# A decoder's feature attention on one Trainium2 core: its products, statistics, stores and loads at other places of a turn, and identity products ahead of stages

## The reference

```python
def _L0_xattn_ref(q, k, v, W):              # q = layernorm(x); k = v = context
    qh = q.reshape(B, H, D, T)              # B 32, H 8 heads, D 8 rows, T 256 features
    kh, vh = ...                            # likewise
    a = jnp.einsum('bhdq,bhdk->bhqk', qh, kh) * D ** (-0.5)
    p = jax.nn.softmax(a, axis=-1)
    y = jnp.einsum('bhqk,bhdk->bhdq', p, vh).reshape(B, C, T)
    return jax.nn.selu(jnp.einsum('oc,bct->bot', W, y))
...
x = x + _L0_attn_ref(_layernorm(x), ...)                 # differential attention
x = x + _L0_xattn_ref(_layernorm(x), ctx, ctx, L0_xattn_W)
x = x + _L0_ffn_ref(_layernorm(x), ...)                  # selection; with the next one: one stage
x = x + _L1_attn_ref(...)                                # state space
x = x + _L1_xattn_ref(...)                               # grouped attention
x = x + _L1_ffn_ref(...)                                 # mixture of experts
```

## Time and profile before

| | us |
|---|---|
| median of three runs | 1376.31 (1371.81 to 1380.15) |
| the profiled execution, its own time | 1374.74 |
| its span, first to last instruction | 1373.0 |
| differential attention | 252 |
| feature attention | 242 |
| selection and state space | 176 |
| grouped attention | 401 |
| mixture | 302 |

### The profile page before, as it was taken

The page is one execution under the profiler, slowest core; times in us unless marked ns, Lnnn a source line. Parts: engine busy times, 40 slices in busy tenths (PEclk is TensorE's granted clock), DMA queues, the critical chain, the costliest instruction groups (busy, mean ns, idle before and its releaser), DMA issues. The chain is left out here.

```text
span 1373.0 us, 27662 instructions
## 1 busy us (share of the span) xinstructions
PE 1233.1 (90%) x9996; PEld 969.6 (71%) x9996; DVE 984.6 (72%) x1869; ACT 704.0 (51%) x1457; POOL 455.3 (33%) x537
## 2 busy tenths in 40 slices
PE   3999998799888957889779999999997799999998
PEld 3776766243333346779658888887876799999998
DVE  4799987688888647788568677777776648555555
ACT  1565655288778835300255656566664363333332
POOL 1333543144554223456562323232422111112210
PEclk9999999699999989899899999999999899999999
DMA  5111026114333130000400000000000300000001
GB/s 178 31 28 35 25 64 136 28 53 110 86 98 94 36 110 1 1 0 0 137 11 4 8 4 8 4 8 4 7 1 0 93 24 25 24 24 24 2 1 62
DMA packets 64927, 54.52 MB, mean 40 GB/s; under 512 B 9192, under 2 KB 56904, under 8 KB 64456
## 3 DMA queue, kind: packets, MB, share of 16 engines
q1 hardware_dynamic: 64846, 53.42, 13.9%
HBM read 38.32 MB, written 14.68 MB: 39 GB/s over the span
## 5 line engine op out<-in xcount | busy, mean ns | idle before, releaser
L783 DVE TENSOR_REDUCE fa_neg_max<-psum 128x2 f32<-128x512 f32 x256 | 161.8, 684 | 26.6 <-PE psum L950 25.7
L838 ACT ACTIVATE fa_probs<-psum 128x1024 f32<-128x1024 f32 x128 | 130.9, 1024 | 37.0 <-PE psum L955 36.8
L1802 PE MATMUL psum<-mo_xT_high,mo_w_high 128*128 128x256 f32 x512 | 145.6, 284 | 2.4 <-DVE mo_xT_low L2630 2.2
L1802 PE MATMUL psum<-mo_xT_low,mo_w_high 128*128 128x256 f32 x512 | 145.2, 284 | 0.0
L1802 PE MATMUL psum<-mo_xT_high,mo_w_low 128*128 128x256 f32 x512 | 144.6, 282 | 0.0
L2462 ACT ACTIVATE mo_silu<-psum 128x256 f32<-128x256 f32 x128 | 49.0, 384 | 155.0 <-PE psum L1802 155.0
L2596 DVE TENSOR_TENSOR mo_mid<-mo_silu,psum 128x256 f32<-128x256 f32 x128 | 53.6, 419 | 92.9 <-ACT mo_silu L2462 92.8
L950 PE MATMUL psum<-stacks_k_stack,stacks_q_stack 48*128 48x256 bf16 x512 | 95.6, 287 | 22.3 <-DVE fa_neg_max L783 15.5
L1802 PEld LDWEIGHTS psum<-mo_xT_high,mo_w_high 128*128 128x128 f32 x512 | 97.4, 190 | 3.0 <-DVE mo_xT_low L2630 2.6
L1938 POOL TENSOR_TENSOR ga_probs<-ga_probs,ga_top 128x1024 f32<-128x1024 f32 x16 | 30.5, 1905 | 205.7 <-DVE ga_top L2092 205.7
L1802 PEld LDWEIGHTS psum<-mo_xT_low,mo_w_high 128*128 128x128 f32 x512 | 97.5, 190 | 0.0
(11 more groups left out here) (419 smaller groups left out, 3586.8 us busy)
## 6 DMA issues: line engine op xcount, KB each, us to landing
k_parts<-da_k_parts SPq DMA_DIRECT2D x96, 64.0 KB, 2.0
q_parts<-stacks_parts SPq DMA_DIRECT2D x96, 64.0 KB, 2.0
stacks_q_stack<-q_parts SPq DMA_DIRECT2D x32, 192.0 KB, 4.0
stacks_k_stack<-k_parts SPq DMA_DIRECT2D x32, 192.0 KB, 3.3
x<-in_x SPq DMA_DIRECT2D x4, 512.0 KB, 5.7
da_context<-in_ctx SPq DMA_DIRECT2D x4, 512.0 KB, 7.8
fa_context<-in_ctx SPq DMA_DIRECT2D x16, 128.0 KB, 2.2
staged<-in_ga_w_q SPq DMA_DIRECT2D x1, 2048.0 KB, 10.5
```

The source lines that it names most:

```text
L783: nc.vector.tensor_reduce(neg_max[:, b, :, head_at(h)], ps[:, h % 2, :].rearrange("p (q k) -> p q k", q=2), AX.X, ALU.max, negate=True).th ...
L838: nc.scalar.activation(probs[:, g].rearrange("p h k q -> p h (k q)"), ps[:, 2 + 2 * (g % 2):4 + 2 * (g % 2), :], ACT.Exp).then_inc(exp_don ...
L1802: done = nc.tensor.matmul(out, lhsT[i], rhs[j], start=start and k == 0, stop=stop and k == 2)
```

## The change

Seven things change, five of them in the feature attention:

1. SP's queue in a turn: context, maxima rows of tile t (second half), then the **stores** of tile t + 3, then the maxima rows of tile t + 1 (first half), then the **loads** of tile t + 2.
2. Queries are stored once per part, three DMAs instead of six, and loaded with three DMAs per lane (of 24, 16 and 8 rows), six instead of two. The keys keep six stores and two loads. The stack in SBUF is the same. The first four tiles, in the differential attention, are stored and loaded likewise.
3. PE: the output product one pair of heads later, the second mixing product one pair of heads later, `turn_mixed(t, 0)` one pair of heads later. ACT's reading of the output product and its copy for `turn_mixed` move with them; ACT now also waits for POOL's selu sum of the turn before.
4. DVE: the statistics one turn later and within the maxima, `normalise` behind the turn's first two maxima, `divide(t, 0)` two maxima later.
5. New: `keep_clock`, products of the identity with itself into a PSUM bank that is overwritten before it is read: 6 ahead of the state-space stage's first transposes, 5 ahead of the grouped attention's, 11 and 14 ahead of the query transposes of its tiles 0 and 1, and in the mixture 5 ahead of its first transposes and 4 behind them.

```diff
+def keep_clock(core, bank, count):
+    for _ in range(count):
+        core.nc.tensor.matmul(core.psum[:, bank, 0:P], core.ident[:], core.ident[:], start=True, stop=True)
...
     def load_q(self, sp, tile, slot, done):
-        self.load(sp, "q_parts", self.q_stack, tile, slot, done)
+        of = self.dram["q_parts"][:, bass.ts(tile, 2 * C_HEADS), :].rearrange("p (b l h) f -> p b l (h f)", b=2, l=LANES)
+        for lane in range(LANES):
+            first = LANE * lane
+            for a in range(PARTS):
+                count = (PARTS - a) * C_HD
+                sp.dma_start(self.q_stack[first:first + count, slot].rearrange("p b h f -> p b (h f)"), of[0:count, :, lane]).then_inc(done, 16)
+                first += count
...
             def store(t, slot):
                 sp.wait_ge(split_done, t + 1)
-                for term, a in enumerate(Q_TERMS):
-                    stacks.store(sp, "q_parts", t + 3, term, parts[:, slot, a]).then_inc(stored[slot], 16)
+                for a in range(PARTS):
+                    stacks.store(sp, "q_parts", t + 3, a, parts[:, slot, a]).then_inc(stored[slot], 16)
...
                 if valid(t):
                     max_to_stack(t, ring(0), 1)
+                if valid(t + 3) and started(t, 1):
+                    store(t, ring(3))
+                if valid(t + 1):
+                    max_to_stack(t + 1, ring(1), 0)
                 if valid(t + 2) and started(t, 2):
                     load(t, ring(2), rounds(2))
-                if valid(t + 1):
-                    max_to_stack(t + 1, ring(1), 0)
-                if valid(t + 3) and started(t, 1):
-                    store(t, ring(3))
...
-                if valid(t + 3) and started(t, 1):
-                    dve.wait_ge(split_done, t)
-                    ln.normalise(rows[:], t + 3).then_inc(rows_ready, 1)
                 for b in range(2):
                     for g in range(4):
...
+                        if g == 0 and b == 0 and valid(t + 3) and started(t, 1):
+                            dve.wait_ge(split_done, t)
+                            ln.normalise(rows[:], t + 3).then_inc(rows_ready, 1)
                         if g == 1 and b == 0 and valid(t - 1):
                             divide(t - 1, 1)
-                        if g == 1 and b == 1 and valid(t):
+                        if g == 2 and b == 0 and valid(t - 2):
+                            row_stats(t - 2)
+                        if g == 2 and b == 1 and valid(t):
                             divide(t, 0)
-                if valid(t - 1):
-                    dve.wait_ge(x_ready, t)
-                    nc.vector.bn_stats(core.row_stats[:, t - 1, :], core.x[:, t - 1, :]).then_inc(stats_done, 1)
...
+                if valid(t):
+                    exponentials(t, 1, 0)
                 if valid(t - 1):
                     act.wait_ge(projected, t)
+                    if started(t, 2):
+                        act.wait_ge(selu_sum, t - 1)
...
                 if valid(t):
-                    exponentials(t, 1, 0)
+                    exponentials(t, 1, 1)
                     take_mixed(t, 0)
...
                     mix(t, ring(0), 0, 0)
+                heads(1, 0)
                 if valid(t - 1):
                     pe.wait_ge(mixed_c_ready, t)
                     nc.tensor.matmul(ps[:, 7, E:2 * E], w_out[:], mixed_c[:], start=True, stop=True).then_inc(projected, 1)
-                heads(1, 0)
+                heads(1, 1)
                 if valid(t):
                     mix(t, ring(0), 0, 1)
-                heads(1, 1)
...
                     turn_max(t + 1, 0)
+                heads(1, 2)
                 if valid(t):
                     turn_mixed(t, 0)
-                heads(1, 2)
...
+            keep_clock(core, SPANS_BANK, 6)
             turn_rows(0)
...
             def turn_queries(n, g):
+                if isinstance(n, int) and n < 2 and g == 0:
+                    keep_clock(core, 4, 11 + 3 * n)
...
+            keep_clock(core, 2, 5)
             turn_x(0)
+            keep_clock(core, 2, 4)
```

25 lines of the change are left out of this document (14 added, 11 removed).

## The result

| | before | after |
|---|---|---|
| median of the runs, us | 1375.93 (1371.81 to 1380.15, 4 runs) | 1452.01 (1450.36 to 1456.02, 4 runs) |
| profiled execution, us | 1374.74, span 1373.0 | 1451.05, span 1449.2 |
| mean granted clock | 0.963 | 0.941 |
| feature attention, us | 243.1 | 322.5 |

The change makes the kernel slower: ratio 1.0567, 95% interval 1.0548 to 1.0587, some 76 us. The forecast was 1416 us with a range of 1390 to 1444, so the sign was right, the result lies above the range, and the cost is nearly twice what I had worked out.

What follows compares the result with a forecast made beforehand. DVE was taken to set the feature attention's pace, waiting on PE and POOL. From 1374.7 us, +50.4 for load waits, -5.2 for moves in four turns and -4 for identity products gave 1416 us, range 1390 to 1444.

Steps and rivals of the forecast that it cites:

- M: Moment in a feature-attention turn when SP issues the maxima rows of the next tile's first half, after waiting for ACT's copy.
- wait for the loads, 12 turns: Feature attention, turns 3 to 14: PE's first score product waits 4.2 us per turn for late key and query loads, +50.4 us.
- S: Start of a feature-attention turn on PE, its first score product; 2.81 us after M in the kernel before.
- moves in turns 0, 1, 2, 15: Feature attention, turns without the wait: moved instructions save 1.3 us of DVE idle time each, -5.2 us in all.
- landing of the last load: Feature attention: the sixth query load, issued at M + 4.84, lands 2.2 us later like the context load, at M + 7.04.
- sum by bytes: Feature attention cross-check: the same bytes took 5.3 us from first key issue to last landing before, giving M + 7.0.
- upper end: Feature attention: if the last load lands like 192 KB loads, 3.9 us, it is there at M + 8.7, a 5.9 us wait.
- clock term: Feature attention, 12 waiting turns: PE starts at 1.2 GHz after the wait, costing 1.3 us, which eats the moves' saving.
- rival 3: Feature attention: wait shorter, turns start with DVE and ACT work done, clock holds; 2.2 us a turn, 1392 us, chance 0.08.
- Rival 2: Feature attention: wait 5.9 us and PE longer at 1.2 GHz, 7.1 us a turn, 1455 us; chance 0.14 with all above 1435.
- Rivals 1, 3 and 4: Feature attention: 1, loads land in time, 1352 us (0.06); 3, shorter wait, 1392 (0.08); 4, small loads land serially, 1522 (0.01).
- What would show it: Feature-attention profile signs: PE waits about 4 us, turns about 18.3 us, M to S 7, S to M 11.4, clock below 1.

## Why the prediction was wrong in size

The right part: the place of the loads behind M, the engine and the turns that wait (PE's first product of turns 3 to 14, 12 times, released by `stacks_q_stack<-q_parts`), the half clock behind each wait, and the identity products. The terms one by one, from the profiled executions (measured 1451.05 - 1374.74 = +76.3 us; forecast +41.3):

| term | forecast, us | measured, us |
|---|---|---|
| wait for the loads, 12 turns | 12 x 4.2 = +50.4 | 12 x 5.5 = +66 |
| S to M in those turns (moves and clock) | 0 | 12 x 1.0 = +12 |
| moves in turns 0, 1, 2, 15 | -5.2 | about 0 |
| identity products | -4 | -4.4 by the ratio, -3 in the trace |

The step that failed is the price of the wait for the loads, and with it the claim that the low clock and the moves cancel: 4.2 + 0 us a turn were forecast, and 5.5 + 1.0 were measured. The measured terms add up to 75 of the 76.3 us.

1. **The landing of the last load was the mis-sized term of the wait.** I took 2.2 us from the context load of the earlier trace rows, since it is the nearest in size. That row is of a DMA that has no such load just ahead of it; the same context load, right behind 768 KB, took 4.0 us in the kernel before with the new order. The last of the six starts where I said (M + 4.84; 370.8 - 365.97 = 4.8), but PE goes on only 3.3 us later. The sum by bytes that I set beside it, 5.3 us from the first key issue, gave the same 7.0 and so looked like a confirmation. It used the median landing of query loads (3.9), where the same loads behind M took 4.3, and an issue at M + 1.68, where SP issued at M + 1.9; from the first key issue to S it was 374.15 - 367.87 = 6.3 us. The run with two large loads (8.0 us) and the one with the keys ahead (6.3 us) show that the amount moved behind M sets the end. My upper end, 5.9 us, did hold it.

2. **The clock term was right in kind and too small.** I priced it at one mixing product and two pairs of heads, 1.3 us. With the clock kept at 1.00 by identity products, S to M was 1.9 us shorter in the trace, and the turn 1.55 us by the runs. All of the first 5 us behind S are at 1.2 GHz, as this window of the kernel before with the new order has it, and there every product on the path is slower, the turned maxima and turned mixing too:

```profile
373.30:378.40 5.10, 5.09 (x40) 2.53 (x42) 2.58 (x4) 2.82 (x4) 0.00 (x0) 0.50 0.00 0
```

The rule that I quoted from the Trainium skill (TensorE: Matmul & The Clock Gate, "Why this matters for your kernels": no idle gaps between bursts of matmuls) agrees with this in direction; the size is the runs'.

3. **The moves were the step that failed in kind.** I counted idle time of DVE as time to be won: 0.91 us ahead of the statistics, 0.9 us behind the output product. In the kernel before both were slack of an engine that waits for PE again right after; taken away, they came back as waits for products (32.5 us in all became 32.9 and 32.0). And I priced the output product's old place without asking what it covered: the landing of the second half's maxima rows, late behind six stores on SP. In the waiting turns the moves give next to nothing either: S to M is 12.5 us without them (the kernel before with the new order) and 12.4 with them. That a waiting turn at full clock needs only 10.5 us, where a turn before needs 11.4, is therefore not shown to be their work. These turns start with the work of DVE and ACT done, as rival 3 has it, and no run parts the two. In the turns without a wait the moves alone gave nothing, and with the small DMAs 0.4 us in the middle turns.

4. **The rivals.** Rival 2, which shared a chance of 0.14 with all above 1435, is what happened. Its two parts were put at 7.1 us a turn, and 20.67 - 14.07 = 6.6 were measured. That its 1455 is only 3 us off is in part luck: the sum leaves the -4 of the identity products out, and still counts -5 for moves that gave nothing. I held the DMA share of 0.27 in the earlier trace rows against it. That is a mean over the stage, and says nothing of the 4 us in which all loads are in flight: in the wait of the kernel with identity products the share is 0.65. Rivals 1, 3 and 4 are out: the wait is longer, not shorter, the clock doesn't hold, and six small loads overlap as well as two large ones. Of rival 3 one half stays: a turn that starts late and at full clock does run to M in less than 11.4 us.

5. **What would show it.** Waits, turns and the lost clock came at their places, with M to S 8.2 to 8.45 and not 7, S to M 12.4 and not 11.4, turns of 20.7 us and not 18.3. DVE's wait for POOL ahead of the statistics is gone but for one at the stage's end. The gap behind the output product did fall, to 0.29 us and 0.65 us:

```profile
382.89 2.54 DVE L795 TENSOR_REDUCE fa_neg_max<-psum 128x2 f32<-128x512 f32 x4 [0.29 <-PE psum L968]
386.08 1.29 DVE L795 TENSOR_REDUCE fa_neg_max<-psum 128x2 f32<-128x512 f32 x2 [0.65 <-PE psum L968]
...
395.65 0.69 DVE L795 TENSOR_REDUCE fa_neg_max<-psum 128x2 f32<-128x512 f32 x1 [6.59 <-PE psum L968]
```

The last of these rows shows DVE's 6.59 us of idle time while PE waits for the loads, beside which such gaps are small.

## What to carry to other kernels

In an in-order DMA queue, what is put behind an issue that waits for a compute engine inherits that wait: here one reordering of three groups of issues cost 5.6% of the kernel, and the number of DMAs nothing. Price a transfer that becomes urgent by all the bytes in flight with it, from its first issue to the start of its consumer, not by the landing of a lone DMA of its size; and where the wait leaves TensorE idle for as long as here (5 to 6 us), add the slower clock behind it as a cost of its own, for about 5 us of its work. An engine's idle time is a gain only if nobody else is late at the next hand-over: before moving an instruction, ask which wait it covers.

## What the runs showed of the hardware

- Filling TensorE's wait with products that nobody reads made the kernel faster by 18.6 us (1452.0 to 1433.4), with M to S at 8.2 us in the traced turn of either (8.5 against 8.2 in the mean of eleven). Behind 5.13 us of idle PE, in the kernel before with the new order, the stretch to 378.40 was granted 0.50; behind 5.6 us of identity products in the same place, the turn was granted 1.00.
- With 30 of them in place of 24 nearly all of this was gone (1448.9 us): they ended 1.2 us behind the time at which the loads were there, in each of 12 turns, and one turn of the trace lost 6 us more without a cause that the profile names.
- 768 KB were there for PE 6.1 us after the first key issue in four loads (367.20 to 373.31), and 6.3 us after it in eight (367.87 to 374.15). A context load of 128 KB right behind the four landed in 4.0 us, and in 2.2 us in the kernel before.
- The same small query load let PE go on 3.3 us after its issue with 384 KB of keys just ahead of it, 2.5 us without. It isn't a fixed time: in the traced turn with 24 identity products SP issued the six more slowly (3.12 us from 362.28), the last one started at about 365.0, M + 5.7, and PE went on at M + 8.2 all the same.
